# Cross-attention and a LoRA feed-forward on one core: q and k on even and odd partitions, two K tiles side by side, x of the first chunk added from SBUF

## The reference

```
q = rope(layernorm(x) @ Wq);  k = rope(ctx @ Wk);  v = ctx @ Wv      # per row of the batch, 128 positions
logits = 30 * tanh(0.0884 * (q . k) / 30);  masked;  w = softmax(logits)
x = x + (w @ v) @ Wo
h = layernorm(x)
x = x + h @ W_base.T + b_base + 2 * sum over the top 2 of 8 experts (weight * (h @ A_e.T) @ B_e.T)
```

## Time and profile before

| | |
|---|---|
| median of three runs | 2150.35 us |
| the profiled execution | 2158.16 us |
| its span in the profile | 2156.4 us |
| TensorE busy | 2132.3 us, 99% |
| VectorE, ScalarE, GpSimd busy | 78%, 41%, 14% |
| SP's DMA queue, GpSimd's DMA queue | 62.7%, 9.3% of 16 engines |

### The profile page before, as it was taken

One profiled execution on the slowest core, in us unless ns is written; L12 is line 12 of the kernel. 1 busy time (PEld: TensorE's weight loads), 2 busy tenths in 40 slices (PEclk: granted clock), 3 DMA queues, 4 the chain that ended last, 5 costly groups with the idle time before them and its releaser, 6 DMA issues.

```text
span 2156.4 us, 26390 instructions
## 1 busy us (share of the span) xinstructions
PE 2132.3 (99%) x9429; PEld 1729.3 (80%) x9429; DVE 1674.3 (78%) x2571; ACT 883.1 (41%) x1342; POOL 294.0 (14%) x359
## 2 busy tenths in 40 slices
PE   9999999999999999998999999999999999999999
PEld 7888888888888888876777877777787777888887
DVE  6976888888886666676877779997999879857443
ACT  3323243222241111155565556655666556423221
POOL 0350001111131000012101111111112111100000
PEclk9999999999999999999999999999999999999999
DMA  8698697665596665698666885689767965696741
GB/s 327 234 332 290 218 334 271 231 221 211 209 339 229 211 212 201 221 279 263 189 193 196 233 224 174 202 273 276 194 195 221 298 182 163 210 368 265 294 184 66
DMA packets 207987, 508.50 MB, mean 236 GB/s; under 512 B 20720, under 2 KB 54128, under 8 KB 205808
## 3 DMA queue, kind: packets, MB, share of 16 engines
q1 hardware_dynamic: 187376, 443.31, 62.7%
q0 software_dynamic: 20480, 63.50, 9.3%
HBM read 357.26 MB, written 149.16 MB: 235 GB/s over the span
## 4 chain that ended last, share of the span: by engine, by line
PE 87%; DMA 7%; DVE 3%; ACT 1%; issue 1%; SPq 0%; POOL 0%; DVEq 0%; ACTq 0%
PE ps L377 28%; PE ps L378 28%; PE ps L379 28%; DMA RB<-rD 3%; DMA rD<-r 2%; PE ps L920 1%; DMA X2D<-stg 1%; DMA raw<-gran 1%; DVE Y L990 1%; DMA Y<-xT 1%; DVE Rl L330 1%; DVE ps L330 0%; DVE ps L905 0%; DVE Pl L330 0%; DMA kraw<-ctxT 0%
## 5 line engine op out<-in xcount | busy, mean ns | idle before, releaser
L377 PE MATMUL ps<-Ah,Rh 128*128 128x512 f32 x1024 | 400.9, 391 | 4.2 <-DVE Y L990 4.2
L378 PE MATMUL ps<-Al,Rh 128*128 128x512 f32 x1024 | 399.9, 391 | 0.0
L379 PE MATMUL ps<-Ah,Rl 128*128 128x512 f32 x1024 | 399.5, 390 | 0.0
L379 PE MATMUL ps<-Xq,qW 128*128 128x512 f32 x896 | 348.6, 389 | 0.0
L377 PE MATMUL ps<-Xq,qW 128*128 128x512 f32 x896 | 348.5, 389 | 0.0
L378 PE MATMUL ps<-Xq,qW 128*128 128x512 f32 x896 | 348.5, 389 | 0.0
L330 DVE TENSOR_TENSOR Rl<-raw,Rh 128x1024 fp32r<-128x1024 f32 x174 | 212.2, 1220 | 57.6 <-ACT Rh L326 57.2
L326 ACT ACTIVATE Rh<-raw 128x1024 fp32r<-128x1024 f32 x176 | 185.5, 1055 | 154.6 <-PE ps L379 127.1
L377 PEld LDWEIGHTS ps<-Ah,Rh 128*128 128x128 f32 x1024 | 193.2, 189 | 46.8 <-DVE Y L990 4.6
L379 PEld LDWEIGHTS ps<-Ah,Rl 128*128 128x128 f32 x1024 | 193.1, 189 | 40.8
L378 PEld LDWEIGHTS ps<-Al,Rh 128*128 128x128 f32 x1024 | 193.2, 189 | 40.5
(11 more groups left out here) (217 smaller groups left out, 3881.7 us busy)
## 6 DMA issues: line engine op xcount, KB each, us to landing
raw<-gran SPq DMA_DIRECT2D x177, 512.0 KB, 5.6
QSD<-qW SPq DMA_DIRECT2D x64, 512.0 KB, 3.1
qD<-qt SPq DMA_DIRECT2D x128, 256.0 KB, 3.3
qW<-QSD SPq DMA_DIRECT2D x64, 512.0 KB, 3.7
qf<-qD SPq DMA_DIRECT2D x64, 512.0 KB, 8.5
RB<-rD POOLq DMA_DIRECT2D x128, 256.0 KB, 6.8
qraw<-gran SPq DMA_DIRECT2D x48, 512.0 KB, 4.3
kD<-kst SPq DMA_DIRECT2D x32, 512.0 KB, 3.8
```

Of the source, the lines that this page charges most:

```text
L377: put("pe", waits, lambda e: e.matmul(pe_out, lh, rh, start=first, stop=False, skip_group_check=more))
L378: put("pe", [], lambda e: e.matmul(pe_out, lh, rl, start=False, stop=False, skip_group_check=more))
L379: return put("pe", [], lambda e: e.matmul(pe_out, ll, rh, start=False, stop=last, skip_group_check=more), mark)
```

## The change

Five edits in three places. `att_load_qk` puts half s of a head's rows on partitions s, s + 2, s + 4 and so on, for q and for k alike. At the start the second granule of K is also loaded in two halves, and a new function `k_both` makes both jobs of the first chunk together: for each k tile of the context three matmuls for the first halves and three for the second, into two banks; the constants `cs` are loaded only when the last piece of the first chunk's context has its high part. For the first group of chunk 0, `o_evac` copies the projected tile from PSUM to Y on ScalarE, and a flex addition then adds Y2, into which x of chunk 0 is loaded at the same point at which it was loaded into Y.

```diff
-        d_c = dma(cs[:, :], cst, [], "d_cst", 196)
...
+        def k_both():
+
+            got = [bank() for _ in k_first]
+            for k in range(KC):
+                for w, (b, waits) in enumerate(got):
+                    lh, ll = KW.tiles(w, k)
+                    m = three(ps[b][:, :], lh, ll, cX[0][:, k, :], cX[1][:, k, :], k == 0, k == KC - 1,
+                              (KW.marks[w] + waits if k == 0 else late[w] if k == 4 else []) + buf_marks["X"][k],
+                              cn("pe_job") if k == KC - 1 else None)
+                    got[w] = b, m if k == KC - 1 else waits
+            last_job[0] = m
+            return got
...
-        k_first = [0]
-        KW.marks[0], first_late = KW.split2(gran[GK], kRh[0][:, :], kRl[0][:, :])
-        KW.n = 1
-        KW.free[0] = None
+        k_first, late = [0, 1], {}
+        for w in k_first:
+            KW.marks[w], late[w] = KW.split2(gran[GK + w], kRh[w][:, :], kRl[w][:, :])
+            KW.free[w] = None
+        KW.n = 2
         ctx_load(0, "X", KW, [1, 2, 3])
-        k_first.append(KW.granule(gran[GK + 1]))
         ctx_load(1, "A", KW)
         gate = buf_marks["A"][-1]
+        d_c = dma(cs[:, :], cst, buf_marks["X"][-1][0:1], "d_cst", 196)
...
+                    if cp + j + i == 0:
+                        first, second = k_both()
+                        pending.append(lambda first=first, second=second: k_evac(0, 0, [first])(second))
+                        continue
...
-            f_marks[gi] = [dma(qf[n][64 * s:64 * s + 64, :, :], qD[c, g, s].rearrange("h p t -> p h t"),
+            f_marks[gi] = [dma(qf[n][s:P:2, :, :], qD[c, g, s].rearrange("h p t -> p h t"),
...
-            k_marks[gi] = [dma(f(kT[n][64 * s:64 * s + 64, :, :]), kD[c, s, :, g].rearrange("l p t -> p l t"),
+            k_marks[gi] = [dma(f(kT[n][s:P:2, :, :]), kD[c, s, :, g].rearrange("l p t -> p l t"),
...
+                if (c, g) == (0, 0):
+                    a = put("act", [m] + y_free[n // 2], lambda e: e.activation(y, ps[b][:, :], ACT.Copy), cn("act_o"))
+                    bank_free[b] = [a]
+                    y_acc[c, n] = [tt("flex", y, y, Y2[:, n, :], ALU.add, [a, y_marks[c, n // 2]], "y")]
+                    y2_free.append(y_acc[c, n][0])
+                    return
...
-                        y_load(0, j)
+                        y_marks[0, j] = dma(Y2[:, 2 * j:2 * j + 2, :], xT[0][:, 2 * j:2 * j + 2, :], y2_free, f"d_y{j}", 512)
```

More of the change, by code:

```diff
@@ L468, in job @@
                     m = three(ps[b][:, :], lh, ll, bh[:, k, :], bl[:, k, :], k == 0, k == KC - 1,
-                              (KW.marks[w] + waits if k == 0 else first_late if k == 4 and w == 0 else []) + buf_marks[buf][k],
+                              (KW.marks[w] + waits if k == 0 else []) + buf_marks[buf][k],
                               cn("pe_job") if k == KC - 1 else None)
```

## The result

The changed kernel takes 2130.05 us (median of 4 runs, 2129.65 to 2131.45); the kernel before, on the same chip, 2151.63 (4 runs, 2149.82 to 2153.23). The ratio is 0.9901, 95% interval 0.9884 to 0.9918: faster, by about 21.6 us. The profiled execution took 2131.45 us, its span is 2129.7. That is 26.7 us less than the profiled execution of before, where 23.8 were forecast.

What follows compares the result with a forecast made beforehand. TensorE, busy 2132.3 of 2156.4 us, bounds the kernel; only its gaps and the slow clock after them can be won. 17.0 + 5.3 + 1.5 = 23.8 us, giving 2126.5 to 2134.3, middle 2130; own range 2125 to 2136.

Steps and rivals of the forecast that it cites:

- Part 1: q and k loads on even and odd partitions: 377 GB/s instead of 208, TensorE's gaps go; 17.0 us, bounds 0 and 17.0.
- the seven gaps: TensorE's idle stretches at 937.14, 966.92, 981.28, 1011.40, 1273.06, 1737.39 and a third wait of 0.8 us.
- a steady share near 0.53: Sign for the faster loads: DMA busy share in the steady part (1100 to 1200) falls from 0.64 to near 0.53.
- Part 2: Gap at 1011.40: x of chunk 0 added from SBUF after ScalarE copies; 5.3 us, bounds 1.0 and 5.9.
- the case that was priced: First ScalarE copy stands behind the waiting Rh; TensorE still waits some 0.6 us, without a slow clock.
- Part 3: Program start: two K tiles side by side, constants loaded after ctx; 1.5 us, bounds -0.5 and 2.5.
- The chunk ends: Sign for the faster loads: denominator transfers r and rD near their medians (2.3 and 1.7 us) there.
- the two cases: Profiled run 7.8 us above the median: difference outside the gaps gives 2126.5 us, gaps widened by profiling 2134.3; middle 2130.
- The first (loads no faster): Rival: stepped q and k loads no faster than 208 GB/s, 2148 us; chance 10%.
- The second (the transfers slow for another reason): Rival: loads faster, but denominator transfers slow through GpSimd's own queue, gaps only halve, 2138 us; chance 15%.
- The third (additions block VectorE): Rival: an addition waiting for its x piece stalls VectorE's in-order queue, x additions give 0, 2135 us; chance 12%.
- The fourth (below 208 GB/s): Rival: neighbouring rows of q and k share ports, rate falls below 208 GB/s, about 2185 us; chance 3%.

Runs made afterwards that it cites:

- the load lines alone: Kernel before with only the q and k loads put on even and odd partitions: 2131.29 us, ratio 0.9892 to the kernel before (2153.57).
- the third set: Four kernels on one chip: the change 2130.21 us, without its x additions 2133.26, without its new start 2131.51, with another start 2130.86; before 2151.95.
- without x: Changed kernel with x of chunk 0 loaded into Y again and added by VectorE's eviction: 2133.26 us, ratio 0.9898 to the kernel before.
- rows in half: Changed kernel, each q and k load cut in two of 32 rows, each staying in one half of the partitions: 2153.89 us, ratio 0.9993 to before.
- rows across: Changed kernel, each q and k load cut in two of 32 rows, each stepping over all 128 partitions: 2134.47 us, ratio 0.9899 to before.

## Why the prediction was right, point by point

- **Part 1, the mechanism.** Shown. The q window moves 401 GB/s at best, about what was taken for its rate (377); six of the seven gaps are gone and 0.54 us is left of the seventh; the part alone has nearly the whole gain. The sign that a steady share near 0.53 was to give came out as 0.58 in the same 100 us: that stretch holds some more other loads (191 against 182 GB/s), and the longer one fits the forecast (77 against 83 us freed).
- **The places, one by one.** Behind the first 48 products TensorE does the same ones in the same order in the kernel before, the changed kernel and the one with the load lines alone. So the lead over the kernel before (the start of a product there minus its start here) can be read at every product. The table shows by how many us it grows at each place, in the profiled executions:

| place (time in the kernel before) | forecast | the change | load lines alone |
|---|---|---|---|
| start, to 900 | 1.5 | 1.0 | 2.1 |
| 937 | 0.8 | 1.1 | 1.0 |
| 967 | 4.1 | 4.3 | 4.3 |
| 981 | 2.2 | 1.7 | 2.5 |
| 1011 | 5.3 | 5.1 | 1.6 |
| 1240 | 0 | 0.7 | 1.0 |
| 1273 | 4.4 | 5.3 | 5.3 |
| 1505 | 0.8 | 1.9 | 1.9 |
| 1737 | 4.7 | 5.6 | 5.6 |
| sum | 23.8 | 26.7 | 25.3 |

- **Part 1, its size: 17.0 us** was some 3 us too small. At its places the changed kernel gains 20.6 (1240 included), the load lines alone 21.6. What the list left out lies at the ends of the chunks: a late exp splits the eight denominator products, which otherwise run as one row of 1.06 us, and the two that are left take another 1.04 us of their own, so each such place costs about 1 us more than its idle time and its slow stretch. At 1240 that is all there is, without a bracket.

```profile
1239.92 2.02 PE L920 MATMUL ps<-Pf,ones 128*32 128x512 f32 x8
...
1269.30 1.06 PE L920 MATMUL ps<-Pf,ones 128*32 128x512 f32 x6
...
1474.61 1.06 PE L920 MATMUL ps<-Pf,ones 128*32 128x512 f32 x8
```

The times alone are less sharp: 22.3 by itself (2153.57 - 2131.29; the interval of its ratio makes that 16 to 31), and 21.7 - 3.0 - 1.3 = 17.4 from the third set, if the parts add.
- **Part 2: 5.3 us** is right for the place and too much for the part. The lead grows by 5.1 at 1011, but the faster loads alone already bring 1.6 of it, which the prediction booked here as the weight load that lands sooner; 3.5 are left for the additions in these executions, 3.0 by the times, and nothing that can be measured without fast loads. The sum doesn't change by that. What is left of the gap without this part differs: 2.52 us and a slow stretch with the load lines alone, 2.48 and none without x. The order came out better than the case that was priced: the first copy was put behind the waiting Rh, with 0.6 us still to wait; it came ahead of it (991.00 before 998.48), and no wait was left. The weight load was expected 2.2 to 2.8 us sooner; issue to use took 12.5 us (985.98 to 998.48) instead of 14.4, 1.9.
- **Part 3: 1.5 us** forecast, 1.3 by the medians, by a course that differs in the details and from execution to execution. In this one K's second tile was ready 0.76 us later than worked out (the products start again at 10.26, not 9.5), one more stop of 0.49 came at 20.08, and the full clock came at 13.76 instead of 17.99, which the prediction had called possible. In the second profiled execution of the same kernel the products start again at 8.98. The prediction also says that only the first two or three microseconds and the seven places have gaps; its own show stops up to 11.88.
- **The chunk ends.** r and rD were to come near their medians there. Only rD did in part: GpSimd's timeline after shows rD issued at 1238.12 and RB, which waits for it, at 1242.03, so 3.9 us from issue to issue instead of the 7.95 of the earlier trace rows (1253.72 to 1261.67); r, issued at 1229.04, is still slow, as rD can follow only at 1238.12. It was enough, since the chain needed 2.7 to 3 us.

```profile
1229.04 0.71 POOL L323 DMA_DIRECT2D r<-rT  x1 [10.66 <-ACT rT L944]
1238.12 0.55 POOL L323 DMA_DIRECT2D rD<-r  x1 [8.36 <-DVE r L948]
1242.03 1.10 POOL L323 DMA_DIRECT2D RB<-rD  x2 [3.36 <-DMA rD<-r]
```

- **The sum, and the offset.** The profiled difference was 26.7 against 23.8; the medians differ by 21.6. The profiled execution of before lay 6.5 us above its median, that of after 1.4 above, so the excess seems to have lain mostly in the gaps. Whether profiling widened them is not shown: 2158.16 also lies well within the runs of the kernel before in the other sets (2143.83 to 2169.23). The middle between the two cases was a guess that turned out well. That 2130 was hit to 0.1 us is luck: the forecast took 20.4 us off a median of 2150.35, and 21.6 came off one of 2151.63.
- **The rivals.** The first (loads no faster) falls with the 401 GB/s; rows in half is what it would have looked like. The second (the transfers slow for another reason) falls at its conclusion, not wholly in its premise: RB still takes 6.71 us and r at the chunk end stays slow, but the gaps don't halve, they go. The third (additions block VectorE) is not seen: none of the eight additions waited for its piece of x; the first two ran without a bracket of idle time. The fourth (below 208 GB/s) is refuted by the same window as the first.

```profile
1003.11 1.28 DVE L330 TENSOR_TENSOR Y<-Y,Y 128x512 f32<-128x512 f32 x2
```

## What to carry to other kernels

Where the DMA share is near 1.0 and the GB/s are half of what other stretches move at the same share, look at which partitions each load reaches before looking at sizes or queues; a load of 64 rows that steps over all 128 partitions is one instruction, like one that fills a half, and took, here, a little over half of its engine time (401 GB/s at a share of 1.04 against 208 at 0.93). With 32 rows to a load the gain was nearly as large. In a stretch that is full of transfers, a wait taken away by reordering can be given back at the next transfer, so free the DMA time first. Idle time in brackets is not all that a wait costs: compare the starts of the same product in two kernels. And when two edits act on one gap, price the second by what the first leaves of it.

## What was not expected of the hardware

- The kernels with fast loads repeat within 2 to 5 us (4 to 6 runs each), while the kernel before and those with loads into half of the partitions spread over 7 to 25 (10 to 25 runs each). Part of that is the number of runs (four runs of the kernel before spread over 3.4), but the gaps that go with a share of 0.76 seem to differ from one execution to the next.
- Gaps of 2.06 us (rows across, at 975.90), 2.41 and 2.52 (the load lines alone) were followed by a stretch at the lower clock of 1.2 GHz, gaps of 2.22 and 2.48 us (without x) were not. A gap's length alone did not decide here whether the clock fell; what did stays open.

```profile
975.90 0.47 PE L376 MATMUL ps<-Ph,vT 128*128 128x512 f32 x1 [2.06 <-DVE Al L330]
```

- A load into half of the partitions keeps the DMA engines' busy share at 0.93 with 208 GB/s, where one into all of them moves 377 at 1.00 and the stepped one 401 at 1.04. The share alone does not tell the two apart.
